# Chunk 1 of the first weights asked for in two requests instead of one

## What is computed

```python
base = jnp.einsum('btd,od->bto', x, W)              # W: 512 x 512
logits = jnp.einsum('btd,ed->bte', x, Wr)           # 8 experts
logits = logits + bias[:, None, :]                  # 5.0 on the expert of the sequence
topw, topi = jax.lax.top_k(logits, 2)
weights = jax.nn.softmax(topw, axis=-1)
gates = jnp.sum(jax.nn.one_hot(topi, E) * weights[..., None], axis=-2)
h = jnp.einsum('btd,erd->bter', x, A)               # 8 x 16 low-rank rows
lora_out = jnp.einsum('bter,bte,eor->bto', h, gates, B)
return x + base + 2.0 * lora_out
```

## Time and profile before

| | us |
|---|---|
| median of 3 runs | 80.47 |
| lowest, highest | 80.07, 80.56 |
| the profiled execution's own time | 80.74 |
| its span in the profile | 78.9 |
| PE busy | 75.4 (95% of the span) |
| VectorE busy | 48.8 (62%) |
| ScalarE busy | 22.1 (28%) |
| GpSimd busy | 22.6 (29%) |

### The profile page before, as it was taken

The page is one execution under the profiler, slowest core; times in us unless marked ns, Lnnn a source line. Parts: engine busy times, 40 slices in busy tenths (PEclk is TensorE's granted clock), DMA queues, the critical chain, the costliest instruction groups (busy, mean ns, idle before and its releaser), DMA issues.

```text
span 78.9 us, 1629 instructions
## 1 busy us (share of the span) xinstructions
PE 75.4 (95%) x505; PEld 71.4 (90%) x505; DVE 48.8 (62%) x220; ACT 22.1 (28%) x56; POOL 22.6 (29%) x26
## 2 busy tenths in 40 slices
PE   6999999999999999999999999999999999999960
PEld 2388799899999999999999999999999999999950
DVE  0095695888892828466482928275664829787750
ACT  4423961244231414050231314140503214112100
POOL 4032926061550241406050513305060605100000
DMA  1999995389199289999930000270000053031133
GB/s 12 293 263 362 412 425 237 40 324 408 37 252 423 121 224 428 423 282 349 411 143 6 0 0 0 97 302 0 0 0 0 0 249 149 0 133 77 60 133 133
DMA packets 3892, 14.23 MB, mean 180 GB/s; under 512 B 432, under 2 KB 1328, under 8 KB 3632
## 3 DMA queue, kind: packets, MB, share of 16 engines
q1 hardware_dynamic: 3744, 13.98, 48.4%
q10 hardware_dynamic: 144, 0.20, 0.7%
HBM read 9.99 MB, written 4.19 MB: 180 GB/s over the span
## 4 chain that ended last, share of the span: by engine, by line
PE 87%; DMA 7%; SPq 1%; ACT 1%; DVE 1%; issue 0%
PE heads_ps L421 43%; PE base_ps L421 28%; DMA first_sb<-in_first 7%; PE heads_ps L453 5%; PE base_ps L453 5%; PE base_ps L457 2%; PE heads_ps L457 2%; PE ghT_ps L444 2%; ACT x_hi L231 1%; SPq L165 1%; DVE out_sb L337 1%; SPq L164 0%; PE warm_ps L444 0%
## 5 line engine op out<-in xcount | busy, mean ns | idle before, releaser
L206 POOL TENSOR_TENSOR x_lo<-xT_sb,x_hi 128x512 fp32r<-128x512 f32 x14 | 18.1, 1294 | 38.8 <-ACT x_hi L241 37.0
L421 PE MATMUL heads_ps<-w_hi,x_hi 128*128 128x392 f32 x64 | 22.8, 366 | 0.2 <-ACT x_hi L231 0.2
L421 PE MATMUL heads_ps<-w_hi,x_lo 128*128 128x392 f32 x64 | 21.6, 348 | 0.0
L421 PE MATMUL heads_ps<-w_lo,x_hi 128*128 128x392 f32 x64 | 21.1, 339 | 0.0
L421 PE MATMUL base_ps<-w_hi,x_lo 128*128 128x256 f32 x64 | 17.8, 281 | 0.0
L421 PE MATMUL base_ps<-w_hi,x_hi 128*128 128x256 f32 x64 | 17.8, 289 | 0.0
L421 PE MATMUL base_ps<-w_lo,x_hi 128*128 128x256 f32 x64 | 17.4, 280 | 0.0
L287 DVE TENSOR_TENSOR ghT_lo<-ghT_ps,ghT_hi 128x128 fp32r<-128x128 f32 x15 | 4.4, 291 | 14.8 <-ACT ghT_hi L245 14.7
L421 PEld LDWEIGHTS heads_ps<-w_hi,x_hi 128*128 128x128 f32 x64 | 12.0, 192 | 1.2 <-ACT x_hi L231 0.7
L421 PEld LDWEIGHTS heads_ps<-w_hi,x_lo 128*128 128x128 f32 x64 | 12.0, 191 | 0.5 <-POOL x_lo L210 0.5
L245 ACT ACTIVATE ghT_hi<-ghT_ps 128x128 fp32r<-128x128 f32 x15 | 4.1, 275 | 29.5 <-PE ghT_ps L444 29.5
(11 more groups left out here) (43 smaller groups left out, 92.2 us busy)
## 6 DMA issues: line engine op xcount, KB each, us to landing
x_sb<-in_x SPq DMA_DIRECT2D x4, 768.0 KB, 5.5
out<-out_sb SPq DMA_DIRECT2D x4, 768.0 KB, 4.4
xT_sb<-in_xT SPq DMA_DIRECT2D x3, 768.0 KB, 4.3
first_sb<-in_first SPq DMA_DIRECT2D x3, 454.0 KB, 5.8
xT_sb<-in_xT SPq DMA_DIRECT2D x1, 1024.0 KB, 6.3
x_sb<-in_x SPq DMA_DIRECT2D x1, 1024.0 KB, 9.6
out<-out_sb SPq DMA_DIRECT2D x2, 256.0 KB, 2.0
out<-out_sb SPq DMA_DIRECT2D x4, 128.0 KB, 1.7
```

Of the source, the lines that this page charges most:

```text
L206: nc.gpsimd.tensor_tensor(x_lo[:, s, :], xT_sb[:, t - len(FIRST), :], x_hi[:, s, :].bitcast(FP32), ALU.subtract).then_inc(x_lo_made, 1)
L421: return nc.tensor.matmul(dst, xs[:, s, chunks[k]], ws[:, k, cols], start=(k == 0 and n == 0), stop=(k == KC - 1 and n == last_n))
```

## The change

The request for chunk 1 becomes two. The first has the 652 numbers of x, ids and heads weights (128 rows of 2,608 bytes, 334 KB in thousands) and keeps the semaphore `chunk_landed[0]`. The second has the 256 numbers of base weights (128 rows of 1,024 bytes, 131 KB in thousands) and has a new semaphore, `wb1_landed`. ScalarE waits for the new one before it makes the base columns of w_hi of chunk 1. No other engine's code is changed.

```diff
+        wb1_landed = sem("wb1_landed")
...
             sp.dma_start(w_sb[:, 0, base_cols], w[:, 0, base_cols]).then_inc(wb_landed, 16)
-            for k in range(1, KC):
+            x_and_heads = slice(0, FIRST_X + IDS + HEADS)
+            sp.dma_start(first_sb[:, 1, x_and_heads], first[:, 1, x_and_heads]).then_inc(chunk_landed[0], 16)
+            sp.dma_start(w_sb[:, 1, base_cols], w[:, 1, base_cols]).then_inc(wb1_landed, 16)
+            for k in range(2, KC):
                 sp.dma_start(first_sb[:, k, :], first[:, k, :]).then_inc(chunk_landed[k - 1], 16)
...
             for k in range(1, KC):
                 act.wait_ge(chunk_landed[k - 1], 16)
                 chunk_upper(k)
-                w_upper(k, base_cols if k == 1 else all_cols)
+                if k == 1:
+                    act.wait_ge(wb1_landed, 16)
+                    w_upper(k, base_cols)
+                else:
+                    w_upper(k, all_cols)
```

## The result

| | before | after |
|---|---|---|
| median, us | 80.35 | 80.02 |
| lowest to highest, us | 79.88 to 80.99 | 79.40 to 80.35 |
| runs | 22 | 22 |
| the profiled execution's own time, us | 80.74 | 79.78 |
| its span, us | 78.9 | 78.0 |

The ratio of after to before is 0.995, with a 95% interval of 0.993 to 0.9971: 0.33 us faster by the medians, clear of no change. In two later sets on other occasions the unchanged text of the change gave 0.9969 [0.994, 0.9999] and 0.9929 [0.9894, 0.9963].

What follows compares the result with a forecast made beforehand. PE, busy 75.4 of 78.9 us, was taken as the bound, with chunk 1's landing setting its start. Landing 0.30 us earlier, with every other cost covered, took 80.47 to 80.17; range 79.80 to 80.70.

Steps and rivals of the forecast that it cites:

- The path of before: Start of chunk 1: its landing, ACT's x_hi, POOL's x_lo for two tiles, then PE; chunk 1 takes 2.42 us, undisturbed 1.77.
- The first part lands 0.30 earlier: Chunk 1's inputs and heads weights: 131 thousand fewer bytes ahead save 0.32 us, less 0.02 for shorter rows; landing at 6.49.
- PE is free for it: PE before chunk 1: chunk 0 ends at 7.02, just ahead of chunk 1's new start at 7.03.
- The added wait on ACT costs nothing: ACT before chunk 1's base w_hi: held at most 0.05 us, ready at 7.29, wanted by PE at 7.46.
- 0.07 more for all behind: DMA queue behind chunk 1: later requests land 0.07 us later, chunk 2 at 7.99, all covered.
- The skill's rule: The added request: about 2.0 us fixed per DMA if paid serially, kernel about 0.9 us slower; the prediction took 0 by overlap.
- early: Chunk 1's first part lands near 5.5 to 6 because single rows stall; gain 0.53 us, 79.94; chance 0.14.
- binding w_lo of chunk 2: Chunk 2's base columns on DVE: w_lo ready at 10.71 plus 0.05 for PE, capping the gain at 0.53 us.
- Nothing: Chunk 1's first part lands no earlier, as both requests' rows are served side by side or delay comes later; 80.47, chance 0.14.
- slower: The second request takes its own queue slot of 1.13 us, delaying base weights and chunk 2; 0.1 to 0.5 slower, 80.8; chance 0.12.

Runs made afterwards that it cites:

- the late base weights: The change with chunk 1's base-weight request moved behind chunk 2's in the queue, against the kernel before: 80.41 against 80.38 us, ratio 1.0037.

## Why the prediction was right

The direction and the size were right: 0.30 us were forecast, 0.33 measured, at 80.02 within 79.80 to 80.70. Of the 0.15 between 80.17 and 80.02, 0.12 is the kernel before, whose median over 22 runs is 80.35 and not 80.47. The path was right too. That the size came out so close was in part luck, as the profiles show: the profiled execution was forecast at 80.44 with chunk 2 at 9.45, and was 79.78 with 8.75. Point by point:

- **The path of before** runs over the landing, ACT, POOL twice and PE: right, and stronger than stated, since three executions follow it to 0.02 us.
- **The first part lands 0.30 earlier:** mis-sized. In three profiles each, x_hi starts at 6.26 to 7.04 before and at 5.70 to 5.81 after, 0.9 on the average of these and 0.65 against the typical execution of before (a median of 80.35 less 73.9 puts it at 6.45). I had scaled bytes, and for an ordinary DMA engine that is about right. The trace keeps sixteen reports of each request, as many as there are DMA engines: the eighth came at 5.10 to 5.12 in the three profiles of before and at 4.81 to 4.92 in those of the change, 0.2 to 0.3 earlier. But the landing is the sixteenth, and that came at 6.24, 6.79 and 7.02 before and at 5.68 to 5.79 with the change. So the part of the step that I left out is the delay of the last engines. Whether the split shortens it, or these three executions were lucky, stays open: the same first request has its last report at 6.35 in the profile with seven warm-ups, when fifteen were in by 5.00.
- **PE is free for it, "this just fits":** this is the term that took part of the larger step back. I took chunk 0's end at 7.02 for a floor on the start of chunk 1 alone and worked on from POOL's chain. The floor also holds for chunk 2, at 7.02 + 1.78 = 8.80, and in executions in which PE's rate rises late it is 9.0. From a typical 9.35 before, this leaves 0.35 to 0.6. So two errors of opposite sign met in the sum: a landing that moved two to three times as far in the profiles, and a floor that took some of it back. The median of the change (80.02, chunk 2 at about 9.02) lies at the low end of that gain, and half its executions are slower still. If the same sums hold for these, they had a later landing or a later end of chunk 0 than the profiles show. If it was the landing, the typical step was nearer to the forecast than the profiles say.
- **The added wait on ACT costs nothing:** right, though it holds ACT for 0.04, 0.14 and 0.10 us in the three profiles and not for at most 0.05; all of it is covered, and the late base weights show what it would have cost.
- **0.07 more for all behind:** wrong in sign where it could be seen. Chunk 2's x_hi starts at 7.30 to 7.38, and before at 7.93, 7.51 and 8.19. It had no effect, as it was covered.
- **The skill's rule** (The Trainium skill, DMA: Bandwidth & Descriptors, Anatomy of one DMA and Rules for kernel authors) of a fixed 2 us on each DMA, and to coalesce: the section gives the 2 us for requests that GpSimd issues, and these are SyncE's. One added request didn't pay it, three added ones cost 0.7 us in all (1.0088). So the rule's direction shows up at four requests and its size nowhere.
- **The rivals:** "early" has the right landing (5.7 to 5.8), and PE's start at the end of chunk 0 in each profile. Its binding w_lo of chunk 2 was not met, as chunk 2 came early too; the x_lo of tile 1 or chunk 0's end bound instead. "Nothing" and "slower" didn't happen; the late base weights confirm the arithmetic of the second.

## What to carry to other kernels

A request lands when its last engine is done, so the row of averages (bytes by a given time) says little about when a semaphore rises: take the landing from several profiles, and ask separately for what the longest chain needs first. When a landing is brought forward, work out the next floor for every point behind it, not for the first consumer alone. And one profile of each kernel isn't a measurement of a 0.3 us change, here a pair of them showed 1.0.

## What the runs showed of the hardware that was not expected

- The landing of one 454 KB request, the third in SyncE's queue, varied between executions by 0.8 us (6.24 to 7.02), while half of its engines had reported at 5.1 each time. That of the 326 KB one in its place varied by 0.7 over seven profiles (5.68 to 6.35).
- PE's rise from 0.33 to 0.18 us for 392 columns came as early as before 4.7 and as late as after 6.2 us from the span's start, after the same nine warm-up matmuls.
- DVE's copy of 128x392 took 0.61 us beside a POOL subtraction, and 0.36 alone; a cast of 128x2 took 0.67 beside one and 0.17 alone.
- One more wait in DVE's program went with a pause of 0.49 us some 67 us later, at another place; the version with the same count of instructions had none. That the one causes the other was not tried further.
